# Joined scan and experts with deeper buffers, scan planes kept on chip, and the experts' results stored by SyncE

## The reference, cut to what matters

```
h = h + _L1_attn_ref(_layernorm(h), ...)      # in-projection, causal conv, silu,
                                              # A = exp(-|x A|*delta), h_t = A_t h_(t-1) + Bx_t, y = h*z, y @ w_out.T
h = h + _L1_ffn_ref(_layernorm(h), ...)
  qkv = x @ W_qkv + b_qkv                     # 16 heads of 16, softmax attention within an image
  gate = softmax(x @ W_gate + b_gate); top_g, top_i = top_k(gate, 2)
  moe_out = sum over the two chosen experts e of top_g * (x @ W_experts[e] + b_experts[e])
  return attn_out + moe_out
```

## Time and profile before

| | us |
|---|---|
| median of 3 runs | 2097.51 (2096.50 to 2102.67) |
| the profiled execution | 2100.46 |
| its span, first to last instruction | 2098.7 |
| TensorE busy | 1885.3 |
| VectorE busy | 1490.7 |
| GpSimd busy | 982.0 |
| ScalarE busy | 940.6 |

### The profile page before, as it was taken

The page is one execution under the profiler, slowest core; times in us unless marked ns, Lnnn a source line. Parts: engine busy times, 40 slices in busy tenths (PEclk is TensorE's granted clock), DMA queues, the critical chain, the costliest instruction groups (busy, mean ns, idle before and its releaser), DMA issues. The chain is left out here.

```text
span 2098.7 us, 36516 instructions
## 1 busy us (share of the span) xinstructions
PE 1885.3 (90%) x10746; PEld 1183.4 (56%) x10746; DVE 1490.7 (71%) x4148; ACT 940.6 (45%) x2120; POOL 982.0 (47%) x1658
## 2 busy tenths in 40 slices
PE   6997997999899999899997984888687899999997
PEld 5886773333788888577775331777564233333332
DVE  3334896777477776799995886566555988889881
ACT  1112664555122222444442443444342377777777
POOL 3554564555333333333332110576434766666662
PEclk9997999999899999999998996999898699999999
DMA  4331668875100000990002001367684044433420
GB/s 134 115 115 36 156 172 192 169 158 109 46 1 1 1 1 26 413 414 28 1 1 62 8 12 51 96 169 193 181 246 137 23 93 102 95 94 92 94 67 27
DMA packets 242419, 216.72 MB, mean 103 GB/s; under 512 B 117762, under 2 KB 216100, under 8 KB 242116
## 3 DMA queue, kind: packets, MB, share of 16 engines
q1 hardware_dynamic: 232596, 188.26, 33.2%
q0 software_dynamic: 9648, 26.36, 3.8%
HBM read 109.35 MB, written 104.82 MB: 102 GB/s over the span
## 5 line engine op out<-in xcount | busy, mean ns | idle before, releaser
L3035 DVE TENSOR_REDUCE attend_mx<-ps 128x1 f32<-128x512 f32 x512 | 320.2, 680 | 38.8 <-PE ps L2689 35.0
L2832 ACT ACTIVATE attend_w<-ps 128x512 f32<-128x512 f32 x512 | 280.2, 597 | 97.0 <-PE ps L2703 79.1
L2689 PE MATMUL ps<-keep_x,keep_o 96*128 96x512 bf16 x512 | 209.4, 414 | 7.7 <-DVE attend_mx L3035 6.0
L2703 PE MATMUL ps<-keep_o,keep_x 99*128 99x512 bf16 x512 | 191.6, 384 | 2.7 <-ACT attend_w L2832 2.7
L2689 PEld LDWEIGHTS ps<-keep_x,keep_o 96*128 96x128 bf16 x512 | 50.2, 99 | 193.7 <-DVE attend_mx L3035 145.4
L981 POOL TENSOR_TENSOR keep_early<-keep_early,first_causal 128x128 f32<-128x128 f32 x256 | 113.2, 458 | 86.7 <-ACT keep_early L949 85.7
L1003 DVE SCALAR_TENSOR_TENSOR keep_early<-ps,first_causal 128x512 f32<-128x512 f32 (+3 forms) x256 | 113.6, 484 | 48.1 <-PE ps L885 43.7
L949 ACT ACTIVATE keep_early<-ps 128x512 f32<-128x512 f32 (+3 forms) x256 | 98.6, 437 | 85.7 <-PE ps L885 85.5
L2721 PE MATMUL ps<-attend_w,keep_early 128*17 128x512 f32 x1024 | 135.5, 598 | 0.0
L1216 PE MATMUL ps<-mlp_zT,keep_early 128*128 128x128 f32 x1056 | 128.2, 280 | 8.0 <-ACT mlp_zT L1258 8.0
L1216 PEld LDWEIGHTS ps<-mlp_zT,keep_early 128*128 128x128 f32 x1056 | 121.9, 194 | 16.0 <-ACT mlp_zT L1258 16.0
(11 more groups left out here) (397 smaller groups left out, 4427.7 us busy)
## 6 DMA issues: line engine op xcount, KB each, us to landing
sorted<-keep_x SPq DMA_DIRECT2D x3, 14720.0 KB, 75.1
tok_xin<-in_xk SPq DMA_DIRECT2D x64, 256.0 KB, 2.6
qk_parts<-qkv_parts SPq DMA_DIRECT2D x33, 384.0 KB, 3.2
qk_parts<-moe_parts SPq DMA_DIRECT2D x33, 384.0 KB
keep_o<-qk_parts SPq DMA_DIRECT2D x16, 384.0 KB, 4.3
keep_x<-qk_parts SPq DMA_DIRECT2D x16, 384.0 KB, 5.6
moe_zs<-sorted SPq DMA_DIRECT2D x45, 128.0 KB, 2.9
sorted<-moe_zn POOLq DMA_DIRECT2D x42, 128.0 KB, 2.9
```

What stands on the lines that cost most here:

```text
L2689: nc.tensor.matmul(ps[:, MX + i % RING, :], qs[0:R, x.buf(0), h, t * P:(t + 1) * P], ks[0:R, x.buf(0), h, :], start=True, stop=True).then_ ...
L2703: nc.tensor.matmul(ps[:, SC + i % RING, :], ks[:, x.buf(2), HG * g + j, kt * P:(kt + 1) * P], qs[:, x.buf(2), HG * g + j, :], start=True, ...
L2832: nc.scalar.activation(w[:, j, kt % 2, :], ps[:, SC + (HG * k + j) % RING, :], ACT.Exp)\
L3035: nc.vector.tensor_reduce(mx[:, t, k:k + 1], ps[:, MX + (TB * k + t) % RING, :], AX, ALU.max)\
```

## The change

Four groups of edits.
- Planes. The five planes stay on chip in `env.planes` (the same memory that `x` was). pass_ssm_in's stores go there, `pr` with three DMAs instead of one; only time 0 still passes through DRAM. The load of line 1952 and its semaphore are gone. ScalarE begins the pass with an activation that loads the Exp table.
- Token loop. `z` has 10 buffers instead of 6, `parts` 3 instead of 2. Tile 0 makes no parts: `class_rows` in TensorE's list computes its 8 columns of q and k alone, and `keep_class` is one instruction. The waits on `s_p2` before `first_part` are gone. SyncE stores the parts and v of the last two tiles after the first six slots' loads.
- Slots. GpSimd's loop of 69 stores is gone. SyncE stores all 73 results, slot j-8 ahead of load j. `y` is the ten `z` buffers.
- Second image. Its pieces are no longer loaded between slots; two whole loads (7 DMAs each) stand at the start of pass_attend, ahead of and behind `class_rows`.

```diff
-                sp.dma_start(io["ssm"][0:3, rows, 1:SEQ], pr[:, :]).then_inc(s_op, 16)
+                for c in range(3):
+                    sp.dma_start(env.planes[rows, c, 1:SEQ], pr[DS * c:DS * (c + 1), :]).then_inc(s_op, 16)
...
-    NZ, NW, NY, NV = 6, 2, 10, 4
-    LAST = 4
+    NZ, NW, NY, NV, NQ, NS = 10, 2, 10, 4, 3, 6
+    LEAD = 8
...
-            sp.dma_start(x[:, :, :], io["ssm"].rearrange("c r t -> r c t")).then_inc(s_xin, 16)
...
+            def store(j):
+                row = sp.value_load(slot_row[0:1, j:j + 1], min_val=0, max_val=ROWS - P)
+                sp.wait_ge(s_y, j + 1)
+                sp.dma_start(io["sorted"][bass.ds(row, P), :], y[j % NY]).then_inc(s_yout[j % NY], 16)
+
             for j in range(NSLOT):
+                if j >= LEAD:
+                    store(j - LEAD)
+                if j == NS:
+                    for s in (NT - 2, NT - 1):
+                        values_out(s)
+                        parts_out(s)
+                    sp.wait_ge(s_qk, NT - 1)
+                    sp.wait_ge(s_v, NT)
                 row = sp.value_load(slot_row[0:1, j:j + 1], min_val=0, max_val=ROWS - P)
                 past(sp, s_dT, j - NY + 1)
                 sp.dma_start(zs[j % NY], io["sorted"][bass.ds(row, P), :]).then_inc(s_zs[j % NY], 16)
-                if j >= 12 and j % 4 == 0 and j < 44:
-                    piece = (j - 12) // 4
-                    env.heads.load_piece(sp, io, 1, piece // 4, 2 + piece // 4, piece % 4)
-            for j in range(NSLOT - LAST, NSLOT):
+            for j in range(NSLOT - LEAD, NSLOT):
+                store(j)
...
             def first_part(s):
-                past(act, s_p2, s - 1)
-                past(act, s_out[u], 16 * (s // 2))
+                past(act, s_out[u], 16 * ((s - 1) // NQ))
...
-            for j in range(NSLOT - LAST):
-                row = pool.value_load(slot_row[0:1, j:j + 1], min_val=0, max_val=ROWS - P)
-                pool.wait_ge(s_y, j + 1)
-                nc.gpsimd.dma_start(io["sorted"][bass.ds(row, P), :], y[j % NY]).then_inc(s_yout[j % NY], 16)
...
+            heads.load(sp, io, 1, 0, 2)
             sp.wait_ge(s_w, 32)
             class_rows()
+            heads.load(sp, io, 1, 1, 3)
```

More of the change, by code:

```diff
@@ L1645, in batch @@
                     return
-                rows = bass.ds(b * DS, DS)
+                rows = slice(b * DS, (b + 1) * DS)
                 sp.wait_ge(s_z16, n)
-                sp.dma_start(io["ssm"][Z_IN, rows, 1:SEQ], z16[:, :]).then_inc(s_oz, 16)
+                sp.dma_start(env.planes[rows, Z_IN, 1:SEQ], z16[:, :]).then_inc(s_oz, 16)
                 sp.wait_ge(s_xs, MI * n)
-                sp.dma_start(io["ssm"][X_IN, rows, 1:SEQ], xs[0:DS, 0, :]).then_inc(s_ox, 16)
+                sp.dma_start(env.planes[rows, X_IN, 1:SEQ], xs[0:DS, 0, :]).then_inc(s_ox, 16)
                 sp.wait_ge(s_prs, n)
-                sp.dma_start(io["ssm"][0:3, rows, 1:SEQ], pr[:, :]).then_inc(s_op, 16)
+                for c in range(3):
+                    sp.dma_start(env.planes[rows, c, 1:SEQ], pr[DS * c:DS * (c + 1), :]).then_inc(s_op, 16)
             batch(-1)
             sp.wait_ge(s_o0, 48)
-            batch(0)
-            with sp.Fori(1, B) as b:
+            sp.wait_ge(s_oz, 16)
+            sp.wait_ge(s_ox, 16)
+            sp.dma_start(env.planes[:, :, 0:1], io["ssm"].rearrange("c r t -> r c t"), allow_slow_non_contiguous=True).then_inc(s_o0, 16)
+            for b in range(B):
                 batch(b)
+            sp.wait_ge(s_o0, 64)
             sp.wait_ge(s_oz, 16 * (B + 1))
             sp.wait_ge(s_ox, 16 * (B + 1))
-            sp.wait_ge(s_op, 16 * B)
+            sp.wait_ge(s_op, 48 * B)
         @block.tensor
@@ L1904, in pass_experts @@
         b_rep = a.sb("b_rep", [P, E, D])
[L1905 to L1907 removed]
+        zs_6 = a.sb("zs", [P, NS, D])
+        zs = [zs_6[:, i, :] for i in range(NS)] + [zT[:, i, :] for i in range(NY - NS)]
+        y = [z[:, i, :] for i in range(NY)]
         staged = zs_6.rearrange("p n d -> p (n d)")
@@ L2056, in project_v, with class_rows @@
                 last.then_inc(s_v, 1)
+            def class_rows():
+                pe.wait_ge(s_zT, 1)
+                for m in range(4):
+                    for k in range(KD):
+                        last = nc.tensor.matmul(ps[:, QK[0], m * P:m * P + B], wqk[:, k, m * P:(m + 1) * P],
+                                                zT[:, 0, k * P:k * P + B], start=(k == 0), stop=(k == KD - 1))
+                last.then_inc(s_q0, 1)
             def project_qk(s):
-                if s == 0:
-                    pe.wait_ge(s_zT, 1)
-                past(pe, s_rest, s - 1)
+                past(pe, s_rest, s - 2)
+                if s == 2:
+                    pe.wait_ge(s_kq0, 1)
                 for m in range(4):
@@ L2114, in _ @@
                 if i == 1:
+                    class_rows()
                     gate(0)
-                    project_qk(0)
                     project_v(0)
@@ L2160, in _ @@
         def _(act):
-            act.wait_ge(s_xin, 16)
+            nc.scalar.activation(warm[:, :], env.eps[:, :], ACT.Exp)
             scan.wait(act)
@@ L2268, in _ @@
                     scatter(i - 2)
-                if projected(i - 1) is not None:
+                if projected(i - 1):
                     third(projected(i - 1))
```

106 lines of the change are left out of this document (50 added, 56 removed).

## The result

The changed kernel takes 2123.9 us (median of 4 runs, 2118.61 to 2124.39) against 2097.74 for the kernel before, run beside it: ratio 1.0115, 95% interval [1.0092, 1.0137]. It is slower, by 1.2%, at the time forecast. The profiled execution has a span of 2122.4 us, 23.7 more than before.

What follows compares the result with a forecast made beforehand. Before, SyncE's loads, TensorE's multiplies and GpSimd's stores ran at nearly one pace in the slots, a buffer ring bound the token loop; -6.8 -3.3 -16 -6.5 +64.2 -5.1 = +26.5 gave 2127.0 profiled, 2124 us forecast, range 2107 to 2146.

Steps and rivals of the forecast that it cites:

- The slots: Slot stage: SyncE's added stores lengthen it from 105.6 to 169.8 us, a cost of 64.2 us.
- Every instruction counts: 146 steps: SyncE in the slots: 73 loads and 73 stores each cost a full serial step of 1.15 us, 167.9 us.
- The store's step is nearly free: Rival, SyncE's slots: second register read hides under the first issue, a store costs 0.47; +20.0, time 2080 us; chance 0.08.
- Register reads are slowed: Rival, SyncE's slots: slower row-number reads make a step 1.27 us, 17.5 us more, time 2141 us; chance 0.12.
- The ring: Token loop: deeper `parts` and `z` buffers remove ScalarE's waits, GpSimd is late next; gain 16 us, at most 21.
- the discount of a quarter: Token loop: only three quarters of the at most 21 us taken as gain, 16, with TensorE close behind at 8.5.
- The rival that the loop would not get faster: Token loop: the deviation still waits for VectorE or the stores' landing only moves; all 16 us missing, 2140 us; chance 0.13.
- The hand-over: Token loop to slots: SyncE stores the last two tiles' parts after slot 6, so its first read comes 6.5 us earlier.
- The start: Start of the token loop: tile 0 makes no parts, `third` and `remainder` go before the first scatter; gain 3.3 us.
- TensorE gains almost nothing: Start of the token loop: `class_rows` still loads all eight weight blocks, so TensorE's time there hardly falls.
- Planes on chip: Plane stage to DEL: no planes' load to wait for, 5.8 us, plus 1.0 from the last store; together 6.8 us gain.
- End of the pass and pass_attend: GpSimd's drain no longer holds the barrier, gain 5.1 us; the second image's loads in pass_attend stay hidden, 0.

Runs made afterwards that it cites:

- the kept row: The changed kernel, with each block's row number read into a register once, at its load, and kept until its store: 2082.64 us, ratio 0.9903 to the kernel before.
- the fixed address: The changed kernel, with each store going to a fixed address of a separate buffer, results not written back to their rows: 2079.03 us, ratio 0.9888 to the kernel before.
- the reads by four: The kernel with the drain covered, with SyncE reading four blocks' row numbers in one load instruction: 2050.09 us, ratio 0.9775 to the kernel before.
- the column apart: The changed kernel, with the class column's 4-byte values stored in rows 2,052 bytes apart: 2119.07 us, ratio 1.0077 to the kernel before.
- the drain covered: The changed kernel, with 64 blocks stored by GpSimd, the last 9 by SyncE, and class column rows 2,052 bytes apart: 2054.58 us, ratio 0.9787 to the kernel before.

## Why the prediction was right

*The slots* (+64.2 forecast, +63.8). "Every instruction counts: 146 steps" held. The step was 1.105 and not 1.15; the four DMAs of the last tiles (3.0 us from the first one's issue to the last one's end, not 1.9) and some slower reads (up to 0.92 us) made up the difference. The assumption behind it, that a step is a serial sum in which a second read hides under nothing, is what the kept row and the fixed address showed: take the read out and 0.64 of the 1.10 us go, at each of the 73 stores. "The store's step is nearly free" was wrong for this kernel, but its price, 0.47 us, is what a store does cost once its row is in a register, and the time it gave (2080) is what those kernels took. "Register reads are slowed" did not come: the median is 270 ns with 121 GB/s about, 292 before with 221. TensorE's lower clock (0.86 in the stage, 0.93 before) was covered, as argued.

The Trainium skill, page DMA: Bandwidth & Descriptors, section Issuing engines are not separate DMA queues, says that issuing from several engines saves only sequencer time, usually little beside the DMA. Here the step took 1.10 us of SyncE against 1.7 from a store's issue to its landing, and moving the stores to another issuing engine was worth 62.7 us of span (2122.4-2059.7). The Trainium skill, same page, section Latency and other measured facts, gives a floor of some 600 ns for a tensor_load. These reads do not show it: the shortest in any of these kernels took 262 ns. Its remark there that the compiler unrolls such loads four times to spread their cost fits the reads by four, which took 7.3 us out of the stage.

*The ring* (-16 forecast, -20.9). The mechanism was right: GpSimd was late next, and a pair of tiles takes 8.8 us (1343.22-1334.40), its own work. The size was the upper bound, since GpSimd waits for VectorE only 0.2 us in the whole loop; the discount of a quarter "with TensorE close behind" had no row behind it. The rival that the loop would not get faster fell. One sign did not come: ScalarE still waits 9.4 us for part stores, off the path by now.

*The hand-over* (-6.5, -9.0). SyncE's part is a little over the forecast (-7.2 from the end of `slots`, bounds were 5 to 7); 1.8 more come because VectorE reaches the end of `slots` sooner after the last scatter.

*The start* (-3.3 forecast, -0.5). This term failed, and the step that failed is "TensorE gains almost nothing". `third` and `remainder` were on the path, as I had said, and their absence gave 1.1 and 1.0 us. But TensorE's stretch up to the gate of tile 1 became 1.6 us longer, at 1.2 GHz where the kernel before was partly at 2.4: its `carry` there took 1.91 us in place of 1.17, and the class's weights 1.80 in place of 1.14, the same matmuls. The prediction has no term for the clock there. No further gain from the one `keep_class` shows.

*Planes on chip* (-6.8 forecast, -3.4 with the row above it). The way to DEL shrank as forecast. The missed part is +3.3 earlier in the plane stage: I costed the stores, but not the small buffer that `ssm` had become. From the last column store to the last `pr` store's first issue are 1282.70-1143.21 = 139.5 us before and 1285.97-1142.36 = 143.6 after; the column's last store lands 3.5 us later after its issue (7.1 against 3.6), and ScalarE's copy waits for it. With the column apart 3.5 of these 4.1 us are gone.

*End of the pass and pass_attend* (-5.1 and 0; -4.9 and -1.3): as forecast.

The errors, +3.3 and +2.8 against -4.9 and -2.5 with small ones, cancel to 2.8 us: the total is better than its parts. The profiled execution was forecast at 2127.0 us and took 2124.33. That the median then agrees to 0.1 us is luck once more: I took off the 2.95 us by which the profiled execution lay above the median before, and after it lies only 0.4 above.

## What to carry to other kernels

Count the sequencer's time of an engine that the page does not list: read, bounds, address and issue follow each other, and work moved to such a queue costs its whole step at the rate at which the stage consumes. If the same row number serves twice, keep it in a register, or read several in one instruction. Of several rings in one loop only the one that binds first pays; deepen the next only behind it.

## What the runs showed of the hardware

- A read of a row number with its bounds check costs SyncE 0.64 us, the issue 0.47, and an address in a register as much as a fixed one. One read of four numbers takes 311 ns in the median, against 270 for a read of one in the changed kernel and 351 in the one with the drain covered.
- The last of five DMAs that store 4-byte values to neighbouring DRAM addresses landed 6.4 to 8.0 us after its issue in nine kernels, and 3.6 to 4.5 in five where the rows are 2,052 bytes apart.
- GpSimd's drain lasts 6.2 to 7.2 us at the end of the two passes in which it issued DMAs, and at most 1.5 in the others. It is 6.67 us even in the changed kernel, where it begins at 1472.4, 9.5 us after the last scatter. Other engines' work can cover it, as long as it starts early enough: with nine stores on SyncE it ended 0.8 us ahead of SyncE, and once SyncE's reads were faster it ended 5 us behind.
